# Fourteen matmuls of a zeroed tile in front of the first transpose of a two-layer transformer kernel

## What is computed

```python
x = x + attn0(layernorm(x))   # 16 query heads, 8 key/value heads of 128; rms-norm and rotation of q and k;
                              # causal mask with a window of 128
x = x + ffn0(layernorm(x))    # silu(x@gate) * (x@up), hidden 1024, the 2 largest of every 4 kept, @down
x = x + attn1(layernorm(x))   # 16 heads of 128, causal
x = x + ffn1(layernorm(x))    # silu(x@W1.T) * (x@W3.T), Walsh-Hadamard transform over 1024, @W2.T
```

## Time and profile before

| | |
|---|---|
| median of 3 runs | 768.96 us (768.14 to 769.33) |
| span of the profiled execution, first to last instruction | 763.1 us |
| PE busy with matmuls, in the span | 712.4 us |
| DVE, ACT and POOL busy | 549.9, 415.8 and 404.2 us |
| mean granted TensorE clock | 0.987 |

### The profile page before, as it was taken

One profiled execution on the slowest core, in us unless ns is written; L12 is line 12 of the kernel. 1 busy time (PEld: TensorE's weight loads), 2 busy tenths in 40 slices (PEclk: granted clock), 3 DMA queues, 4 the chain that ended last, 5 costly groups with the idle time before them and its releaser, 6 DMA issues.

```text
span 763.1 us, 15137 instructions
## 1 busy us (share of the span) xinstructions
PE 712.4 (93%) x4360; PEld 633.9 (83%) x4360; DVE 549.9 (72%) x1861; ACT 415.8 (54%) x1213; POOL 404.2 (53%) x545
## 2 busy tenths in 40 slices
PE   4899999999999969986888999999999999989998
PEld 3589999899899967775776899999999999877887
DVE  7898987988898897979867655555545555576533
ACT  3577777677677754430344556555555655644221
POOL 4898888788787856526387523233241514416000
PEclk9999999999999999988999999999999999999999
DMA  6011010101110110300101010101010100000000
GB/s 220 2 43 32 12 43 2 42 0 41 58 67 0 55 56 1 110 1 1 42 1 56 1 56 1 56 1 55 0 55 0 60 36 14 1 14 1 1 28 28
DMA packets 9015, 24.75 MB, mean 32 GB/s; under 512 B 896, under 2 KB 3072, under 8 KB 8832
## 3 DMA queue, kind: packets, MB, share of 16 engines
q1 hardware_dynamic: 8240, 22.55, 8.6%
q10 hardware_dynamic: 720, 1.57, 0.6%
HBM read 23.07 MB, written 1.05 MB: 32 GB/s over the span
## 4 chain that ended last, share of the span: by engine, by line
PE 80%; DVE 12%; issue 4%; ACT 1%; POOL 1%; DMA 1%; DVEq 0%; SPq 0%; ACTq 0%; POOLq 0%
PE bank L296 11%; PE bank L597 10%; PE bank L279 10%; PE bank L273 10%; PE bank L328 7%; PE bank L251 6%; PE bank L308 5%; PE bank L317 5%; PE bank L630 5%; PE bank L330 3%; PE bank L250 3%; PE bank L339 3%; DVE work L814 2%; DVE probs L414 1%; PE bank L655 1%
## 5 line engine op out<-in xcount | busy, mean ns | idle before, releaser
L500 POOL TENSOR_TENSOR a_hi<-raw_a,zero 128x384 fp32r<-128x384 f32 (+2 forms) x75 | 60.4, 805 | 116.7 <-PE bank L308 115.0
L431 DVE TENSOR_TENSOR enc_lo<-bank,enc_hi 128x256 fp32r<-128x256 f32 x128 | 54.2, 423 | 74.2 <-PE bank L251 66.0
L402 ACT ACTIVATE probs<-scores,negmax,rms_r 128x128 f32<-128x128 f32 (+1 forms) x128 | 69.1, 540 | 61.1 <-DVE negmax L453 61.1
L414 DVE TENSOR_SCALAR probs<-probs,rinv 128x128 f32<-128x128 f32 (+1 forms) x256 | 90.9, 397 | 4.5
L352 ACT COPY probs_t<-bank 128x384 f32<-128x384 f32 x128 | 60.6, 474 | 57.5 <-PE bank L317 56.6
L402 ACT ACTIVATE probs<-scores,negmax 128x128 f32<-128x128 f32 (+1 forms) x128 | 57.2, 448 | 58.0 <-DVE negmax L457 58.0
L447 DVE CUSTOM_DVE_ANT_0 scores<-bank,cst 128x128 f32<-128x128 f32 (+1 forms) x256 | 80.0, 350 | 3.5 <-PE bank L251 3.5
L296 PE MATMUL bank<-b_hi,enc_hi 128*128 128x256 f32 x256 | 73.7, 288 | 9.3 <-DVE x L422 9.1
L328 PE MATMUL bank<-probs_t,v 128*128 128x256 f32 x256 | 77.0, 383 | 2.9 <-DVE enc_lo L431 2.8
L251 PE MATMUL bank<-qk 128*128 128x256 f32 x256 | 76.9, 382 | 0.0
L502 POOL TENSOR_TENSOR a_lo<-raw_a,a_hi 128x384 fp32r<-128x384 f32 (+2 forms) x75 | 72.8, 970 | 5.9
(11 more groups left out here) (106 smaller groups left out, 2216.2 us busy)
## 6 DMA issues: line engine op xcount, KB each, us to landing
raw_a<-in_wa SPq DMA_DIRECT2D x10, 768.0 KB, 4.4
raw_a<-in_wa SPq DMA_DIRECT2D x9, 512.0 KB, 4.4
raw_b<-in_wb SPq DMA_DIRECT2D x16, 256.0 KB, 2.7
x<-in_x SPq DMA_DIRECT2D x4, 256.0 KB, 5.9
w_a<-in_w2t SPq DMA_DIRECT2D x1, 1024.0 KB, 4.8
raw_a<-in_wax SPq DMA_DIRECT2D x2, 512.0 KB, 3.2
raw_b<-in_wdown SPq DMA_DIRECT2D x2, 512.0 KB, 3.8
raw_a<-in_wa ACTq DMA_DIRECT2D x1, 512.0 KB, 4.6
```

Source lines behind the costliest of these rows:

```text
L402: nc.scalar.activation(probs[:, c % 4, c0:c1], scores[:, c % 2, c0:c1], ACT.Exp, bias=negmax[:, c % 2, r:r + 1], scale=scale, accum_out=ro ...
L414: nc.vector.tensor_scalar(probs[:, m % 4, c0:c1], probs[:, m % 4, c0:c1], rinv[:, m % 4, r:r + 1], None, ALU.mult).then_inc(s["pnorm"], 1)
L500: nc.gpsimd.tensor_tensor(hi, src, zero[:, 0:1].broadcast_to(list(src.shape)), ALU.add).then_inc(s_hi, 1)
```

## The change

A bf16 tile of 128 x 512, blank, is added, and a semaphore. DVE sets the tile to zero as its first instruction. PE waits for that and multiplies the tile by its own first 128 columns 14 times, 512 columns each, into bank 0, ahead of its wait for the identity. Nobody reads the result and no one waits for it; the scores of unit 0 overwrite the bank. Nothing is removed or moved.

```diff
+WARM_UP = 14
...
+        blank = sb("blank", [P, 512], BF16)
...
+        s_blank = sem("blank_set")
...
         @block.vector
         def _(dve):
+            nc.vector.memset(blank[:, :], 0.0).then_inc(s_blank, 1)
             for t in (0, 2):
                 dve.wait_ge(s_x[t // 2], 16)
                 ln_dve_stats(dve, 0, t, t + 1)
...
         @block.tensor
         def _(pe):
+
+            pe.wait_ge(s_blank, 1)
+            for _ in range(WARM_UP):
+                pe.matmul(bank[S_BANK][:, :], blank[:, 0:P], blank[:, :], start=True, stop=True)
             pe.wait_ge(s_ident, 16)
             for t in range(4):
                 ln_pe(pe, 0, t, 4 + t)
```

## The result

| | before | after |
|---|---|---|
| median of 20 runs each, same chip | 768.44 us (764.77 to 770.49) | 770.83 us (766.80 to 773.67) |
| span of the profiled execution | 763.1 us | 765.2 us |
| time of the profiled execution | 764.77 us | 766.80 us |
| mean granted TensorE clock | 0.987 | 0.982 |

Ratio 1.0032, with a 95% interval of 1.0018 to 1.0047: the changed kernel is 0.32% slower, some 2.4 us. That lies in the predicted range, near its upper edge, and on the side that was given 0.17; what put the edge there (the matmuls' upper bound of 1.2 us, and rival B) is not what happened, as will be seen. Both profiled executions are the fastest of their twenty. Two things follow. The time around the span is 1.6 to 1.7 us, not the 5.9 of the working ahead of the prediction; the other 4.2 us are what an ordinary execution takes longer than the one that was profiled.

What follows compares the result with a forecast made beforehand. DVE, behind x's load, was taken to bound the head up to 19.7 us, and PE the rest from about 34 us. Four terms of 0 left the span at 763.1 us; 5.9 around it made 769.0, range 767.4 to 771.0.

Steps and rivals of the forecast that it cites:

- the side that was given 0.17: Whole kernel: the outcome slower by more than 0.2% (1.5 us), chance 0.17.
- the matmuls' upper bound: Kernel start: blank matmuls at 0.63 us each take 8.8 us, end by 10.3, and lose 1.2 us.
- rival B: Head: projections 0 and 1 end early, the clock falls, projection 2 runs low; 1.5 to 1.8 us slower, chance 0.18.
- The forecast, A: Head: the blank matmuls are hidden and faster projections save nothing on the chain; 769.0 us, chance 0.66.
- the pace of 0.43 us: Kernel start: blank matmuls taken at 0.427 us each, 6.0 us in all, over by 6.9 to 7.5 us.
- the fall between 9 and 13 us: Head: the clock falls again before or during projections 0 and 1, leaving them mostly at 1.2 GHz; 0 us saved.
- DVE's unbroken row: Head: DVE has no gap from 9.05 to 20.2 us, so faster matmuls there save 0 us.
- DVE's queue is empty until 4.29 us, so it costs nothing: Kernel start: DVE waits for x until then, so the added memset costs 0 us.
- Rival C: Later code: 28 more PE instructions might shift an issue wait onto PE's path, 771.0 us, or remove one; chance 0.05.
- The prediction's last sign: Whole kernel: same head but another time would mean the code's position or the clock's falls after 320 us.
- Rival D: Head: the 12 low-clock matmuls were on the path, 2.4 us faster, or the smaller gain of 1.5 us; chance 0.11.
- D's smaller half: Head: other executions get the clock later and pay for it; ending this gives 1.5 us, 767.5 us.

Runs made afterwards that it cites:

- again: The changed kernel, unaltered, run once more beside the kernel before: 771.70 us median, ratio 1.0036.
- tile_last: The whole change, with the blank tile allocated behind all others so that no other tile moves: 771.24 us median, ratio 1.0034 to the kernel before.
- narrow: The changed kernel with its 14 blank matmuls 8 columns wide instead of 512: 771.77 us median, ratio 1.0025 to the kernel before.
- bridge: The changed kernel with 18 blank matmuls in front and 8 more behind the transposes of tiles 0 to 3: 771.85 us median, ratio 1.0043 to before.
- none: The changed kernel with tile, memset, semaphore and wait but no blank matmul: 769.83 us median, ratio 1.0019 to the kernel before.
- head_none: The kernel with tile, memset and wait but no blank matmul, cut behind slot 10 of the first attention: 70.68 us median.
- head_before: The kernel before, cut behind slot 10 of the first attention: 70.47 us median.
- gap4: The changed kernel without its 14 matmuls, four put behind the transposes of tile 4, blank tile allocated last: 769.03 us median, ratio 1.0012 to the kernel before.
- pool14: The whole change, with the memset as POOL's first instruction instead of DVE's: 768.29 us median, ratio 1.0009 to the kernel before.
- aa: The kernel before, unaltered, measured against itself: 769.22 us median, ratio 0.9999.
- tile: The kernel before with only the blank tile allocated, no memset, wait or matmul: 768.54 us median, ratio 0.9995.

## Why the prediction came out as it did

**The forecast, A: right in the head, wrong in the sum.** The measured median lies inside the stated range, but by luck: its upper edge was drawn from the matmuls' upper bound and from rival B, and neither made the loss. Each of the steps in the head held: the memset, the pace of 0.43 us, the fall between 9 and 13 us, DVE's unbroken row, the waits behind it. The step that failed is "DVE's queue is empty until 4.29 us, so it costs nothing". The cost of the instruction was looked for where it runs. It is paid where DVE's program, one instruction longer, is late by 0.35 us behind a wait (0.33 in this pair of traces), and so comes to its first xn behind POOL: 0.33, 0.66 more for the four xn and 0.63 more for the two enc_lo are the 1.6 us of chain, in every trace with the memset on DVE, with or without the matmuls.

**Rival C had the cause under the wrong engine.** It asked what longer code could do, gave it 0.05, and dismissed DVE with "DVE moves by a single instruction". A single one was enough. The prediction's last sign, the same head and another time, meaning "the code's position or the falls after 320 us", is the one that came. The 28 new PE instructions cost nothing that shows in these traces: DVE's 2.1 us of issue at the loop's first way back are 2.1 us again, and between 66 and 260 us the traces of before and after agree to 0.1 us.

**Rival B is real, and it is not the main cause.** Where the clock fell at about 18.4 to 18.9 us (again, tile_last, narrow, bridge, none), DVE was 0.5 to 1.8 us late at 29 us. Up to 0.5 us of that had come with x, which landed later (0.52 in narrow, 0.33 in again), so the fall costs 0.5 to 1.2 us, less than B's 1.5 to 1.8. It needs no full-width blank matmul (none, narrow), and the profiled execution of the change escaped it. But all five falls are in traces with the memset on DVE, and none in the four others; of the cut kernels, where the mean clock tells of one in three of five executions of head_none and in one of six of head_before, no mean differs. That the change makes the fall more frequent in the whole kernel, and loses some tenths of a us by it, is not ruled out.

**Rival D, and the two pages.** Bridge kept the clock at 2.4 GHz through both projections, and PE waited for DVE instead. D's smaller half, a fall that other executions of before have and the change ends, is not borne out either: the change was slower, and one cut execution of before in six shows such a fall. By the Trainium skill, TensorE: Matmul & The Clock Gate, section Why this matters for your kernels, a TensorE kept busy has its full clock. The traces of bridge (1.00 from 5.4 to 18.8 us, PE busy for 9.10 of the 13.40) and gap4 agree; before's 6.00 us of unbroken work at 0.50 from 354.9 us on the earlier trace rows do not. Gap4's time says that it is worth nothing that could be measured here. The rule on transposes of the same page is neither borne out nor refuted: the clock did fall behind them, at 9.8 us, after a stretch from 7.0 us with 1.6 us of work.

**The numbers.** 769.0 us was the median of before carried over, and it stands for that median; but 5.9 us "around the span" were 1.7 us around it and 4.2 us of luck in the profiled execution. Two sums of the prediction are off by 0.1 us, without effect: the blank matmuls would have had 0.5 to 1.1 us to spare by its numbers (7.99 less 7.5 and 6.9), and rival C's time is 771.1 (769.0 and 2.1). Of the change's loss of 2.5 to 2.8 us (ratios 1.0032, 1.0036 and 1.0034 of 768.5), 1.6 are shown. The 0.85 us of the longer low clock behind it would make 2.45; that it follows from the first was not tried by itself, and the mean clocks of all runs speak against it: twice the lost share times the span is 34.8 us of low clock in the 44 runs of after, again and tile_last, 28.0 without the 6.8 us at the projections that their record begins early enough to hold, and 27.6 in 86 runs of before beside the experiments. The loss that moving the memset takes away is clear of noise on the means: the three measurements of the whole change together lost 2.6 ± 0.3 us and pool14 0.3 ± 0.7, a difference of 2.2 ± 0.8, though the intervals of the single ratios (1.0018 to 1.0047, 0.9989 to 1.0029) overlap. About 1 us stays open. None and gap4, with the memset and few or no blank matmuls, together lost 1.2 ± 0.4 us, 1.4 ± 0.5 less than the whole change. That may be a part of the matmuls, or the clock's fall in the head, or chance; pool14, which has all fourteen, speaks for a small part.

**What is open.** Why DVE's qk starts 0.35 us later when one instruction stands ahead of it is known only in part. The waits in DVE's own program have the same times in all eleven traces, counted from the gate's start: qk's wait ends at 1.37 to 1.40 us (361.34 us in after, 362.15 in pool14), and the next wait, that of the first xn, begins at 1.81 to 1.83. The three waits behind it begin 0.11 us apart, with one instruction between each two; here it is 0.44 us. So DVE's program halts here for some 0.33 us with and without the memset. Without it qk is on its way before the halt and starts 0.04 us behind the end of its wait; with it the halt comes one instruction sooner, and qk starts 0.40 us behind. Read so, the halt belongs to a place in the order of the program, and the memset moved qk to its other side. What the halt is stays open. By the Trainium skill, Runtime: NRT & Kernel Launch, section Instruction fetch mechanics, the code of an engine is fetched in blocks of 256 instructions, and crossing one is mostly hidden; that the halt is such a boundary is a guess that no run here shows. No kernel had two or more instructions added on DVE, which would have told whether it is the place. No version that ran is faster than the kernel before.

## What to carry to other kernels

An instruction that is free where it runs is not free for the program behind it. Look for the places on the chain where two engines start within 0.2 us of each other and the order decides, and put a new instruction on an engine that has none. When a trace of after shows its place of change untouched and the time is not, align the two traces instruction by instruction and ask where the distance steps, and trust a step only if it comes back in other executions.

## What was not expected of the hardware

* Here two DVE operations from SBUF to SBUF, xn and enc_lo, that start behind a POOL operation last until that one is through and a little longer. The xn of 128x256 takes 0.40 us alone. In after POOL's enc_lo runs from 362.19 to 363.49 us and the xn from 362.35 to 363.65. In before and in pool14 the second xn, which starts 0.15 and 0.12 us behind POOL, takes 1.39 us in the same way, and enc_lo of 0.68 us takes 1.47. The Trainium skill, SBUF — State Buffer, section SBUF: two separate sides, has it so for a DVE operation in a two-port mode, or one with two inputs in SBUF while POOL's reads SBUF: whichever of the two engines starts first has the shared port pair for its whole instruction, and the other blocks. The traces agree, as far as xn runs in such a mode, which they don't show; enc_lo has its two inputs in SBUF, and so has POOL's.
* The clock's falls differ by several us from execution to execution of one kernel (before against aa, after against again). At about 271 us it fell in nine of the eleven traces: for 3.4 us in five, for 6.8 in tile, for 10.2 in again, tile_last and narrow (2.2 us late from it); in before and after it didn't. Here is that stretch in again:

```profile
271.00:281.00 10.00, 8.49 (x32) 7.61 (x33) 6.70 (x22) 3.49 (x11) 7.48 (x8) 0.50 0.26 86
```

  and in before:

```profile
271.00:281.00 10.00, 7.84 (x53) 6.57 (x53) 9.34 (x28) 5.72 (x18) 5.99 (x6) 1.00 0.33 106
```

  Near 427 us the low stretch is 3.4 us long in some and 6.8 in others, and DVE falls back by some 1.6 or 2.8 us there against before. Such steps, and the head's, are as large as the effect that was looked for; the runs of these two kernels scatter from 764.8 to 773.7 us.
* DVE zeroes 128x512 bf16 in 0.27 us, and the record has it as 256 words of 32 bits a partition.
